# A recommender tower on one core: steps 0 and 1 in halves of their columns, part of step 2's first layer on VectorE, unread matmuls at both ends, tile 14's MLP in turn 31

## The chip, the cores and the metric

The kernel runs on one core of one Trainium2 chip. The metric is the device time of the whole kernel in microseconds (us). Before the change it is 1184.62 us, the median of three runs (1183.82 to 1184.74).

## What is computed

For each of 2048 samples, 32 rows of 16 numbers are looked up in 32 tables (`e`, 2048 x 32 x 16). Three layers of a compressed interaction network follow: each multiplies every pair of a field of `e` and a feature of the layer before, dimension by dimension, and contracts the pairs with weights to 64 features, with a ReLU. The sums over the 16 dimensions of the three layers, with 16 dense features, go through an MLP (208 to 512 to 256 to 1).

```python
x0 = e; xk = x0
for W in (W0, W1, W2):                       # W0: 32x32x64, W1 and W2: 32x64x64
    xk = relu(einsum('bmd,bhd,mhk->bkd', x0, xk, W))
    outs.append(sum(xk, axis=2))
h = concatenate([*outs, dense_ctx], axis=1)  # 2048 x 208
h = maximum(h @ W_top1 + b_top1, 0)
h = maximum(h @ W_top2 + b_top2, 0)
y = h @ W_top3
```

Everything is in float32.

## The kernel before

**Steps.** The batch is cut into 32 steps of 64 samples. In a step the 64 x 16 values of a field are 1024 columns (`COLS`), of which a matmul takes 512 (`BLK`). Two steps make a tile of 128 samples, for which the MLP runs once.

**Where the rows come from.** GpSimd gathers table rows by indirect DMA, 16 gathers for a step, into `x_rows`. SyncE (SP) stores them twice, one copy behind the other, in a scratch area in HBM (`store_x`, L184) and loads them from there, shifted by a number of fields for each group of 32 partitions: `q_tile` (the plain fields, four times, 0.52 MB) and eight tiles of `spread` (0.52 MB each), the first four with `load_a`, the last four with `load_b`. For step 0 the loads are shared by SP's and ScalarE's queues, and its and step 1's first four tiles each have a semaphore of their own.

**A layer.** All products of pairs are elementwise multiplications: a "chunk" is 128 pairs by 1024 columns. The first layer of a step (layer 0) has five chunks: four are `spread` tiles times `q_tile` (`p_l0`) and one holds the squares, 32 rows, made by ScalarE. Their products are made by VectorE for steps 0 and 1 and by GpSimd from step 2 on (two instructions of two chunks). Layers 1 and 2 have 16 chunks each, `spread` times the features of the layer before. VectorE makes 15 of them in groups of one to three (`GROUPS_L1`, `GROUPS_L2`) into a ring of ten slots (`p_dve`, `RING`), and waits for a slot to be consumed (`dve_used`); GpSimd makes chunk 7 (`p_pool`). TensorE contracts each chunk with two matmuls (`contract`, L624), one for each half of the columns, each with 64 output rows, one in the lower and one in the upper half of the accumulator's partitions. Every float32 matmul shows as two records.

**Between layers.** ScalarE moves the accumulator through a ReLU to `xa` (features in the order of chunks 0 to 7, `relu_a`), `xb` (chunks 8 to 15, `relu_b`), `x_s` (for GpSimd, `relu_s`) and `out_l` (for the sums, which VectorE makes with a reduction). `xa` and `xb` exist once, so that they are written when VectorE has passed the chunks that read them.

**The order.** There is no planner; the order on every engine is written out. Turn s holds layer 1 of step s and layer 2 of step s-1, and, inside layer 2, TensorE's layer 0 of step s+1 behind chunk `L0_AFTER` = 3. Step 1's layer 0 sits in layer 1 of step 0 behind chunk 10, step 2's in layer 2 of step 0 behind chunk 9. GpSimd's chunk is contracted behind chunk 9 (layer 1) or 11 (layer 2), for step 0 behind chunk 14. The MLP of tile t runs two turns and more after the tile's steps; that of tile 14 is placed in layer 2 of step 30 and of step 31. GpSimd's queue in a turn: first-layer products of step s+1, 4 gathers, its product of layer 2, 4 gathers, its product of layer 1 of the next step, 8 gathers. After the first 32 gathers it waits for `x1a_ready`, which says that ScalarE has written `xa` for step 0.

## Time and profile before

| | |
|---|---|
| median of three runs | 1184.62 us (1183.82 to 1184.74) |
| the profiled execution's own time | 1190.19 us |
| its span, first to last instruction | 1188.4 us |
| TensorE matmuls | 1121.7 us (94%), 5312 records |
| VectorE | 1119.2 us (94%) |
| ScalarE | 734.3 us (62%) |
| GpSimd | 913.9 us (77%) |
| loaded and stored | 167.25 MB, mean 141 GB/s |
| mean granted TensorE clock | 0.989 |

The profile is of one execution. PE is TensorE's matmuls, PEld its loads of weights, DVE is VectorE, ACT ScalarE, POOL GpSimd, SP SyncE; SPq and ACTq are DMA issues. Times are us from the span's start, and L542 is line 542 of the kernel. A merged row gives its start, its length, the engine, the line, the operation, the number of instructions, and in brackets how long the engine was idle before it and what ended that. A record of a matmul outlasts the start of the next one.

### The profile page before, as it was taken

What the parts mean: (1) busy time and instruction counts of PE and PEld (TensorE: products, weight loads), DVE (VectorE), ACT (ScalarE), POOL (GpSimd) and SP (SyncE); (2) the same over time, 40 slices, a digit from 0 to 9 for tenths busy, and PEclk for the clock granted to TensorE, in tenths of its full rate; (3) what the DMA queues carried; (4) which work ended last, traced back from release to release, by engine and by line L of the source; (5) the groups of instructions that cost most, each with busy time, mean ns of one, the idle gap of its engine ahead of it and who ended that gap; (6) DMA issues with size and microseconds to landing.
All of it is one profiled execution on the core that took longest, in us unless ns stands there. A gap on an engine that the chain in (4) does not pass through costs nothing.

```text
span 1188.4 us, 14675 instructions
## 1 busy us (share of the span) xinstructions
PE 1121.7 (94%) x5312; PEld 398.0 (33%) x5312; DVE 1119.2 (94%) x525; ACT 734.3 (62%) x1361; POOL 913.9 (77%) x640
## 2 busy tenths in 40 slices
PE   0489899999999999999999999999999999999997
PEld 0132223333333333333333333333333333333343
DVE  0488999999999999999999999999999999999994
ACT  0445667567656756765675676567567666756662
POOL 6568888888888888888888888888888888884300
PEclk9899999999999999999999999999999999999998
DMA  5885788767768876666787666678866667886100
GB/s 114 225 178 118 154 165 173 153 128 148 142 133 163 172 158 144 133 141 140 151 172 160 142 135 141 140 148 172 162 143 137 140 137 149 172 167 140 37 1 1
DMA packets 76472, 167.25 MB, mean 141 GB/s; under 512 B 22032, under 2 KB 39328, under 8 KB 76400
## 3 DMA queue, kind: packets, MB, share of 16 engines
q1 hardware_dynamic: 58704, 159.59, 63.8%
q0 software_dynamic: 16384, 4.23, 3.8%
q10 hardware_dynamic: 1312, 2.50, 0.8%
q8 instruction: 42, 0.69, 0.3%
q14 instruction: 30, 0.25, 0.1%
HBM read 157.86 MB, written 8.40 MB: 140 GB/s over the span
## 4 chain that ended last, share of the span: by engine, by line
PE 84%; issue 6%; DVE 2%; ACT 2%; DMA 1%; POOL 1%; another core or an unknown queue 1%; SPq 1%; ACTq 1%; DVEq 0%; POOLq 0%
PE acc L627 78%; PE acc L700 3%; DVE p_dve L542 2%; PE acc L686 1%; POOL x_rows L260 1%; PE acc L688 1%; DMA q_tile<-x_of_steps 1%; ACT xb L324 1%; PE acc L708 1%; ACTq L466 0%; SPq L197 0%; DMA x_rows<-in_table,ids_s 0%; SPq L225 0%; ACT xa L315 0%
## 5 line engine op out<-in xcount | busy, mean ns | idle before, releaser
L627 PE MATMUL acc<-p_dve,w_s 128*64 128x512 f32 x3840 | 859.6, 596 | 24.2 <-issue 12.7
L260 POOL DMA_INDIRECT x_rows<-in_table,ids_s x512 | 488.4, 954 | 152.5 <-issue 136.3
L542 DVE TENSOR_TENSOR p_dve<-spread,xb 128x3072 f32<-128x3072 f32 (+2 forms) x224 | 573.5, 2701 | 0.0
L542 DVE TENSOR_TENSOR p_dve<-spread,xa 128x2048 f32<-128x2048 f32 (+1 forms) x192 | 502.7, 2749 | 17.5 <-ACT xa L315 14.0
L627 PEld LDWEIGHTS acc<-p_dve,w_s 128*64 128x64 f32 x3840 | 272.1, 137 | 563.1 <-issue 489.4
L324 ACT ACTIVATE xb<-acc 32x512 f32<-32x512 f32 x512 | 288.8, 564 | 23.8 <-DVE p_dve L542 17.4
L272 POOL TENSOR_TENSOR p_l<-spread,q_tile 128x2048 f32<-128x2048 f32 x60 | 272.9, 4575 | 12.3 <-DMA q_tile<-x_of_steps 9.0
L315 ACT ACTIVATE xa<-acc 64x512 f32<-64x512 f32 x256 | 146.1, 571 | 183.9 <-DVE p_dve L542 98.2
L283 POOL TENSOR_TENSOR p_pool<-spread,x_s 128x1024 f32<-128x1024 f32 x64 | 152.4, 2381 | 85.4 <-PE acc L627 43.0
L627 PE MATMUL acc<-p_l,w_s 128*64 128x512 f32 (+1 forms) x640 | 153.1, 613 | 36.7 <-issue 36.7
L333 ACT ACTIVATE x_s<-acc 64x512 f32<-64x512 f32 x256 | 151.7, 593 | 8.2 <-ACT y_row L456 4.8
L342 ACT ACTIVATE p_l<-q_tile 32x1024 f32<-32x1024 f32 x32 | 33.8, 1056 | 116.7 <-DMA q_tile<-x_of_steps 116.7
L627 PEld LDWEIGHTS acc<-p_l,w_s 128*64 128x64 f32 (+1 forms) x640 | 40.9, 137 | 145.7 <-issue 143.7
L569 DVE TENSOR_REDUCE z<-out_l 128x32 f32<-128x512 f32 x96 | 70.0, 795 | 4.5 <-ACT out_l L408 4.5
L627 PE MATMUL acc<-p_pool,w_s 128*64 128x512 f32 x256 | 66.1, 592 | 0.0
L437 ACT ACTIVATE h<-acc,bt 128x128 f32<-128x128 f32 x64 | 18.3, 369 | 33.7 <-remote 25.8
L700 PEld LDWEIGHTS acc<-h,wt 128*128 128x128 f32 x256 | 31.4, 200 | 13.7 <-issue 12.2
L700 PE MATMUL acc<-h,wt 128*128 128x128 f32 x256 | 34.6, 291 | 1.2 <-ACT h L437 1.2
L627 PEld LDWEIGHTS acc<-p_pool,w_s 128*64 128x64 f32 x256 | 18.6, 137 | 36.4 <-issue 36.4
L583 DVE TENSOR_TENSOR p_l<-spread,q_tile 128x1024 f32<-128x1024 f32 x8 | 9.6, 1227 | 20.7 <-issue 19.1
L686 PE MATMUL acc<-z_all,wt 128*128 128x128 f32 x128 | 27.1, 294 | 2.0 <-ACT z_all L414 2.0
L408 ACT ACTIVATE out_l<-acc 128x512 f32<-128x512 f32 x32 | 19.2, 600 | 14.9 <-PE acc L627 14.8
(18 smaller groups left out, 160.2 us busy)
## 6 DMA issues: line engine op xcount, KB each, us to landing
spread<-x_of_steps SPq DMA_DIRECT2D x246, 512.0 KB
q_tile<-x_of_steps SPq DMA_DIRECT2D x126, 128.0 KB
x_rows<-in_table,ids_s POOLq DMA_INDIRECT x512
x_of_steps<-x_rows SPq DMA_DIRECT2D x64, 128.0 KB
spread<-x_of_steps SPq DMA_DIRECT2D x24, 128.0 KB
w_s<-in_w SPq DMA_DIRECT2D x2, 512.0 KB
spread<-x_of_steps ACTq DMA_DIRECT2D x8, 128.0 KB
spread<-x_of_steps ACTq DMA_DIRECT2D x2, 512.0 KB
```

The costliest lines, as they stand in the source:

```text
L260: nc.gpsimd.indirect_dma_start(out=x_rows[:, s % 2, i * DIM:(i + 1) * DIM], out_offset=None, in_=table, in_offset=bass.IndirectOffsetOnAxi ...
L272: nc.gpsimd.tensor_tensor(p_l0[:, c:c + 2, :], spread[:, s % 3, c:c + 2, :], q, ALU.mult).then_inc(l0_made, 2)
L283: nc.gpsimd.tensor_tensor(p_pool[:], spread[:, s % 3, POOL_CHUNK, :], x_s[:, layer - 1, :], ALU.mult).then_inc(pool_made, 1)
L315: last = nc.scalar.activation(xa[to:to + K, b * BLK:(b + 1) * BLK], acc[b * K:(b + 1) * K, :], ACT.Relu)
L324: last = nc.scalar.activation(xb[q * FIELDS:(q + 1) * FIELDS, b * BLK:(b + 1) * BLK], hi if q % 2 == 0 else lo, ACT.Relu)
L333: last = nc.scalar.activation(x_s[to:to + K, layer - 1, b * BLK:(b + 1) * BLK], acc[b * K:(b + 1) * K, :], ACT.Relu)
L342: nc.scalar.activation(p_l0[0:FIELDS, CP, :], q_tile[0:FIELDS, :], ACT.Square).then_inc(squares_made, 1)
L542: nc.vector.tensor_tensor(p_dve[:, to:to + n, :], spread[:, s % 3, tile:tile + n, :], over(x[:], n), ALU.mult).then_inc(dve_made, n)
L569: nc.vector.reduce_sum(z[:, s // 2 % 2, n, s % 2, :], out_l[:, n, :].rearrange("p (i d) -> p i d", d=DIM), AX_X).then_inc(z_made[n], 1)
L627: last = nc.tensor.matmul(acc[b * K:(b + 1) * K, :], w, prod[:, b * BLK:(b + 1) * BLK], start=start, stop=stop)
L686: nc.tensor.matmul(acc0[:, cols], wt1[:, 0, cols], z_all[:, 0, :], start=True, stop=False)
L700: last = nc.tensor.matmul(acc0[:, cols], wt2[:, k, cols], h1[:, k, :], start=(k == 0), stop=(k == H1 // P - 1))
```

## The change

- **Steps 0 and 1 in halves.** Samples are reordered so that the first 8 gathers of these steps bring the first 512 columns. Each half is stored, loaded (`load_half_by`, in rows half as long) and multiplied by VectorE by itself: one instruction for the first half, two for the second. TensorE contracts a half with one matmul per chunk (`layer0_half`), step 1's halves behind chunks 10 and 13. ScalarE squares each half and writes the first half of `xa` when that half is contracted. SP and ScalarE share the loads of step 1's second half and last four tiles.
- **Step 2's first layer.** VectorE makes its chunks 0 and 1 (`first_layer_of_2`), GpSimd chunks 2 and 3; TensorE takes it behind chunk 7 in place of 9.
- **GpSimd's order.** It makes 48 gathers without the wait for `x1a_ready`. Its chunk of layer 1 of step 0 is contracted behind chunk 5 of layer 1 of step 1.
- **Unread matmuls** (`keep_busy`): 4 before, 7 between and 8 behind the halves of step 0, then 4, 2 and 1 ahead of the last tile's three MLP layers.
- **Tile 14's MLP** follows chunks 6 and 12 of layer 2 of step 30 and chunk 1 of step 31. ScalarE collects its sums earlier, and evicts `mlp2` before `x2_b` of step 31.
- The last layer's last two chunks are separate instructions.

```diff
+GROUPS_LAST = [(0, 2), (2, 3), (5, 2), (8, 3), (11, 1), (12, 2), (14, 1), (15, 1)]
-POOL_AFTER_OF_0 = 14
+POOL_AFTER_L1_OF_0, POOL_AFTER_L2_OF_0 = 5, 14
-L0_OF_1_AFTER = 10
-L0_OF_2_AFTER = 9
+L0_OF_1_AFTER = 10, 13
+L0_OF_2_AFTER = 7
-LATE_MLP1_AFTER, LATE_MLP2_AFTER, LATE_MLP3_AFTER = 10, 14, 3
+BUSY_BEFORE, BUSY_BETWEEN, BUSY_BEHIND = 4, 7, 8
+BUSY_AT_END = 4, 2, 1
+LATE_MLP1_AFTER, LATE_MLP2_AFTER, LATE_MLP3_AFTER = 6, 12, 1
...
+        def load_half_by(engine, s, b, quads):
+            cols = slice(b * BLK, (b + 1) * BLK)
+            for q in quads:
+                engine.dma_start(q_tile[q * FIELDS:(q + 1) * FIELDS, cols],
+                                 scratch[s, 0:FIELDS, cols]).then_inc(half_q_loaded[s][b], 16)
+            for i, n, signal in ((0, NA, half_a_loaded[s][0]),) if b == 0 else \
+                    ((0, NA // 2, half_a_loaded[s][1]), (NA // 2, NA - NA // 2, a_loaded[s])):
+                for q in quads:
...
-            gathers(0, 2 * XI)
-            pool.wait_ge(x1a_ready, 1)
-            gathers(2 * XI, 3 * XI)
+            gathers(0, 3 * XI)
             product(0, 1)
             product(1, 1)
-            gathers(3 * XI, GATHERED_IN_TURN_0)
+            gathers(3 * XI, gathers_before(1))
...
+                if s < 2:
+                    for b in range(2):
+                        act.wait_ge(l0_used, 2 * s + b + 1)
+                        relu_a(acc0, x1a_ready, [b])
...
             x2_a(STEPS - 1)
             mlp1(TILES - 2)
+            mlp2(TILES - 2)
             x2_b(STEPS - 1)
-            mlp2(TILES - 2)
             out_2(STEPS - 2)
...
+            def first_layer_of_2():
+                dve.wait_ge(q_loaded, 16 * Q)
+                dve.wait_ge(a_loaded[2], 16 * Q)
+                dve.wait_ge(l0_used, 4)
+                n = CP // 2
+                nc.vector.tensor_tensor(p_l0[:, 0:n, :], spread[:, 2, 0:n, :],
+                                        over(q_tile[:], n), ALU.mult).then_inc(l0_made_by_dve, 2 * n)
...
+            def layer0_half(s, b):
+                if s > 0 and b == 0:
+                    pe.wait_ge(x1b_ready, s)
+                    pe.wait_ge(out_ready[0], s)
+                for c in CP, *range(CP):
...
+                    last = nc.tensor.matmul(acc0[b * K:(b + 1) * K, :], w0_s[0:rows, c, :],
+                                            p_l0[0:rows, c, b * BLK:(b + 1) * BLK],
+                                            start=c == CP, stop=c == CP - 1)
+                last.then_inc(l0_used, 1)
+
+            def keep_busy(acc, n):
+                for _ in range(n):
+                    nc.tensor.matmul(acc[0:K, :], w1_s[:, 0, :],
+                                     wt2[:, 0:BLK // H2, :].rearrange("p k n -> p (k n)"), start=True, stop=True)
...
+            keep_busy(acc2, BUSY_BEFORE)
+            layer0_half(0, 0)
+            keep_busy(acc2, BUSY_BETWEEN)
+            layer0_half(0, 1)
+            keep_busy(acc2, BUSY_BEHIND)
...
+            pe.wait_ge(out_ready[1], STEPS)
+            keep_busy(acc1[0], BUSY_AT_END[0])
             mlp1(TILES - 1)
+            keep_busy(acc1[0], BUSY_AT_END[1])
             mlp2(TILES - 1)
+            keep_busy(acc1[0], BUSY_AT_END[2])
             mlp3(TILES - 1)
```

## Rows read from the trace of the kernel before

**Rows 1.** The page, first part: busy us, share of the span, instructions.
```profile
PE 1121.7 (94%) x5312; PEld 398.0 (33%) x5312; DVE 1119.2 (94%) x525; ACT 734.3 (62%) x1361; POOL 913.9 (77%) x640
```

**Rows 2.** Timeline of VectorE in the middle: start, length, what [idle before].
```profile
598.21 7.86 DVE L542 TENSOR_TENSOR p_dve<-spread,xa 128x3072 f32<-128x3072 f32 x3
...
632.82 7.87 DVE L542 TENSOR_TENSOR p_dve<-spread,xa 128x3072 f32<-128x3072 f32 x3
```

**Rows 3.** Timeline of TensorE in the middle: an MLP layer and four chunks.
```profile
643.99 2.05 PE L700 MATMUL acc<-h,wt 128*128 128x128 f32 x16
...
649.46 3.60 PE L627 MATMUL acc<-p_dve,w_s 128*64 128x512 f32 x16
```

**Rows 4.** Timeline of VectorE, start of layer 1 of steps 0 to 3.
```profile
50.95 7.75 DVE L542 TENSOR_TENSOR p_dve<-spread,xa 128x3072 f32<-128x3072 f32 x3 [9.94 <-ACT xa L315]
...
76.66 7.75 DVE L542 TENSOR_TENSOR p_dve<-spread,xa 128x3072 f32<-128x3072 f32 x3 [4.05 <-ACT xa L315]
...
113.68 7.75 DVE L542 TENSOR_TENSOR p_dve<-spread,xa 128x3072 f32<-128x3072 f32 x3 [3.51 <-issue]
...
148.30 7.75 DVE L542 TENSOR_TENSOR p_dve<-spread,xa 128x3072 f32<-128x3072 f32 x3
```

**Rows 5.** Chain of waits at the end: start, length, what.
```profile
1163.89 10.48 PE acc L627 x48
...
1176.31 0.51 PE acc L686 x2
...
1181.05 3.79 PE acc L700 x16
```

**Rows 6.** Timeline of all engines, 0 to 70 us.
```profile
12.65 0.94 POOL L260 DMA_INDIRECT x_rows<-in_table,ids_s  x1 [0.30 <-issue]
...
22.63 0.94 POOL L260 DMA_INDIRECT x_rows<-in_table,ids_s  x1 [0.30 <-issue]
...
25.01 0.81 SPq L189 DMA_DIRECT2D x_of_steps<-x_rows  x2
...
27.23 0.79 SPq L225 DMA_DIRECT2D q_tile<-x_of_steps  x2
...
34.04 1.23 DVE L583 TENSOR_TENSOR p_l<-spread,q_tile 128x1024 f32<-128x1024 f32 x1 [18.64 <-issue]
...
39.79 1.23 DVE L583 TENSOR_TENSOR p_l<-spread,q_tile 128x1024 f32<-128x1024 f32 x1 [1.18 <-DMA spread<-x_of_steps]
...
43.45 0.14 PEld L627 LDWEIGHTS acc<-p_l,w_s 128*64 128x64 f32 x2 [0.60 <-issue]
...
48.55 2.32 ACT L315 ACTIVATE xa<-acc 64x512 f32<-64x512 f32 x4 [12.30 <-remote]
...
65.33 3.91 PE L627 MATMUL acc<-p_l,w_s 32*64 32x512 f32 x16
```

**Rows 7.** Timeline of ScalarE, 60 to 120 us.
```profile
74.25 2.32 ACT L315 ACTIVATE xa<-acc 64x512 f32<-64x512 f32 x4 [14.75 <-remote]
```

**Rows 8.** Windows: length, busy time per engine, granted clock, DMA share, GB/s.
```profile
57.00:70.00 13.00, 11.97 (x54) 3.56 (x52) 13.00 (x8) 2.48 (x4) 9.95 (x11) 1.00 1.06 212
...
74.10:77.50 3.40, 3.40 (x10) 1.49 (x8) 0.84 (x1) 3.18 (x6) 0.18 (x1) 0.51 0.25 82
...
1176.60:1188.40 11.80, 8.01 (x36) 6.75 (x35) 0.00 (x0) 2.04 (x7) 0.00 (x0) 0.50 0.00 0
```

**Rows 9.** Timeline of GpSimd, its products only.
```profile
79.73 2.37 POOL L283 TENSOR_TENSOR p_pool<-spread,x_s 128x1024 f32<-128x1024 f32 x1 [5.46 <-PE acc L627]
...
131.56 9.07 POOL L272 TENSOR_TENSOR p_l<-spread,q_tile 128x2048 f32<-128x2048 f32 x2
```

**Rows 10.** Timeline of all engines, 1138 to 1176 us.
```profile
1146.80 2.79 PE L627 MATMUL acc<-p_dve,w_s 128*64 128x512 f32 x12 [0.70 <-DVE p_dve L542]
...
1152.78 4.60 ACT L324 ACTIVATE xb<-acc 32x512 f32<-32x512 f32 x8
...
1159.71 3.65 PE L627 MATMUL acc<-p_dve,w_s 128*64 128x512 f32 x16 [0.70 <-ACT out_l L408]
```

More of the change, by code:

```diff
@@ L142, in build_kernel @@
         q_loaded = sem("q_loaded")
-        tile_loaded = [[sem(f"tile{i}_of_step{s}_loaded") for i in range(NA - 1)] for s in range(2)]
+        half_gathered = [[sem(f"half{b}_of_step{s}_gathered") for b in range(2)] for s in range(2)]
+        half_q_loaded = [[sem(f"half{b}_of_step{s}_q_loaded") for b in range(2)] for s in range(2)]
+        half_a_loaded = [[sem(f"half{b}_of_step{s}_a_loaded") for b in range(2)] for s in range(2)]
         a_loaded = [sem(f"a_loaded{u}") for u in range(3)]
@@ L258, in gather @@
                 if i == 0 and s >= 2:
-                    pool.wait_ge(x_stored, 32 * (s - 1))
+                    pool.wait_ge(x_stored, stored(s - 2) if s >= 4 else 64 * (s - 1))
                 nc.gpsimd.indirect_dma_start(
@@ L310, in _, with relu_a @@
         def _(act):
-            def relu_a(acc, signal):
-                for b in range(2):
+            def relu_a(acc, signal, halves=range(2)):
+                for b in halves:
                     for to in 0, K:
@@ L316, in relu_a @@
                                                     acc[b * K:(b + 1) * K, :], ACT.Relu)
-                last.then_inc(signal, 1)
+                if halves[-1] == 1:
+                    last.then_inc(signal, 1)
             def relu_b(acc, signal):
@@ L351, in x1_a @@
                     act.wait_ge(dve_made, dve_from(s - 2, 2) + POOL_CHUNK)
-                relu_a(acc0, x1a_ready)
+                if s < 2:
+                    for b in range(2):
+                        act.wait_ge(l0_used, 2 * s + b + 1)
+                        relu_a(acc0, x1a_ready, [b])
+                else:
+                    act.wait_ge(l0_used, 2 * (s + 1))
+                    relu_a(acc0, x1a_ready)
             def x1_s(s):
@@ L376, in x2_a @@
                 act.wait_ge(dve_used, dve_from(s, 1) + CD)
+                if s == 0:
+                    act.wait_ge(pool_used, 1)
                 if s + 1 < STEPS:
@@ L611, in _ @@
                     for c, n in GROUPS_L2:
+                        if s == 1 and c == L0_OF_2_AFTER + 1:
+                            first_layer_of_2()
                         layer2(s - 1, c, n)
-            for c, n in GROUPS_L2:
+            for c, n in GROUPS_LAST:
                 if c == NT:
@@ L645, in layer0 @@
-                    contract(acc0, w0_s[0:rows, c, :], p_l0[0:rows, c, :], c == CP, c == CP - 1
-                             ).then_inc(l0_used, 1)
+                    if c == CP:
+                        pe.wait_ge(squares_made, 2 * (s + 1))
+                    elif s == 2 and c < CP // 2:
+                        pe.wait_ge(l0_made_by_dve, l0_by_dve(2))
+                    else:
+                        pe.wait_ge(l0_made, l0_by_pool(s) - CP + c + 1)
+                    last = contract(acc0, w0_s[0:rows, c, :], p_l0[0:rows, c, :], c == CP, c == CP - 1)
```

237 lines of the change are left out of this document (141 added, 96 removed).

## The prediction, made before the changed kernel was run

> **What bounds the kernel now.** I read the page's first part, then the timeline of VectorE, then ScalarE's and TensorE's rows at both ends, then GpSimd's. The page names no bound: TensorE and VectorE are both busy 94% of the span [rows 1], and the chain of waits runs mostly over TensorE. The timeline decides it. In the middle VectorE starts layer 1 of one step at 598.21 and of the next at 632.82, so a step lasts 34.61 us, and no row between shows idle time [rows 2]. TensorE needs less: a chunk is four matmul records (two passes of two column halves), and 16 of them take 3.60 us with the overhang of the last, some 0.17, so a chunk costs 0.86 [rows 3]; 37 chunks are 31.8 us, and the MLP adds some 4.5 us per two steps. So VectorE sets the pace, TensorE follows with under 1 us of slack, and GpSimd (16 gathers of 1.25 us, 9.1 us of first-layer products, two products of 2.4 us, some 33.9 us) is nearly full as well. The middle is untouched by the diff, apart from fewer increments of l0_used. What can move is (a) when VectorE enters each of the first layers and (b) what follows its last product.
>
> VectorE enters layer 1 of steps 0 to 3 at 50.95, 76.66, 113.68 and 148.30, with idle times of 9.94, 4.05 and 3.51 before the first three and none after [rows 4]. The last product begins at 1167.99; TensorE ends at about 1174.36, the program 14.0 later [rows 5].
>
> **S, the start of layer 1 of step 0.** Now: the 16th gather is issued at 22.63, its rows are stored at 25.01, loads start at 27.23, the first product at 34.04, the fourth at 39.79; TensorE's last load of weights is at 43.45, and ScalarE begins x1_a at 48.55, 4.2 us after the matmuls should be over (44.3) [rows 6]. This lag is a hold on TensorE's completions: its waits are over and nothing else precedes ScalarE.
> After: (1) first half. The 8th gather (12.65) is 10.0 us before the 16th, so the store is at 15.0, the load at 17.2. 1.05 MB (q and tile 0) took 6.8 us (27.23 to 34.04), the other three tiles of 0.52 MB 5.75, 1.9 each [rows 6]; half of q and of four tiles is 1.31 MB, 6.8 and half a tile more, 7.7 us: 24.9. Its product has 2048 elements, 2.2 us: 27.1. (2) second half. The gathers aren't faster: stored from 25.0, loads from 27.2; 0.79 MB in 5.9, by 33.1, the rest by 35.1, last product at 36.3 (before 41.0). (3) TensorE. A half is ONE matmul per chunk, without a partner in the other column half. The nearest row is the MLP: 8 unpaired matmuls on 128 columns of data in 2.05 us with the overhang [rows 3], under 0.25 each; 512 columns are four times that: 0.86 to 1.0, I take 0.86. So an unpaired half costs what both halves cost now; lower bound 0.43. At half clock it is double, as mlp2 shows at the end (3.79 [rows 5]). First half: four matmuls after 27.1, 3.4 to 6.8 us, to 30.5 to 33.9. Then seven unread ones, in order, 6.0 us: to 36.5 to 39.9, which covers the second half's products. Then five, 4.3: 40.8 to 44.2. I take 42.5: the split and the fillers give back most of the 4.7 us that the loads won. (4) Lag. GpSimd no longer stops for x1a_ready, so gathers and bulk loads run on together, as around 43 us. Bounds 0 and 7.7 (layer 0 of step 1: its first chunk runs at 65.33 and is done by 66.2 [rows 6]; TensorE's records end at 70.9, and ScalarE starts at 74.25 after 14.75 us of waiting [rows 7], so the lag is 3.4 at the last chunk and at most 8.1 less the handover at the first); I take 3.5, near the first row. (5) ScalarE has only half of x1_a left, 1.2 instead of 2.4.
> S = 42.5 + 3.5 + 1.2 = 47.2 (bounds 42.1 and 53), against 50.95.
>
> **From S to step 1 (T).** VectorE alone: 7.7, sum 0.6, 3.3, half of step 1 2.3, 3.3, other half 2.3, 2.2 = S+21.7. TensorE is later: chunks 8 to 10 after S+11.5, to S+14.1; half, five matmuls, to S+18.4; chunks 11 to 13 to S+21.0; half to S+25.3; ScalarE's half 1.2 and handover: T = S+26.8 = 74.0. Now it is 25.7, the same path with lag. The split adds 8.6 us of TensorE in all, and takes VectorE's place here. The 48th gather is issued at 22.63+32x1.25 = 62.6 plus delays, so no gathers and no lag at T. Data: one queue moves 212 GB/s [rows 8]. The last four tiles of step 0 end at about 44.5, then come a store, 1.31 MB to 55, a store, and 1.31 MB by two queues to about 64.7, needed at S+18.3 = 65.5.
>
> **Steps 2 and 3.** The GpSimd chunk of layer 1 of step 0 is read after chunk 5 of step 1, T+9.4, so GpSimd's next product starts at T+9.5, now at T+3.1 (79.73) [rows 9]. Twelve gathers in place of eight; its half of step 2's first layer from T+26.9 to T+31.5 (4.5 saved), VectorE's half 2.2 at T+24.7, behind it (8,3) to (14,2). TensorE has layer 0 of step 2 by T+33.3, ScalarE by T+35.8, VectorE by T+35.6: layer 1 of step 2 at T+35.9 = 109.9 (now T+37.0). A product waits 1.3 for pool_used; first-layer products of step 3 start at T+58.1, now T+54.9 (131.56) [rows 9], while layer 2 of step 1 starts at T+54.1, now T+55.2. Ten slots of the ring then run full: (14,2) wants chunk 5 consumed at T+70.0, ready at T+68.3; stall 1.7 to 2.0. Layer 1 of step 3 at T+72.4 = 146.4, now 148.30: gain 1.9. GpSimd's own turn is 33.5, so it catches up and nothing more is lost.
>
> **End.** mlp1 of tile 14 goes after chunk 6 (1146.1), where TensorE is idle 0.70 until 1146.80: to 1148.1; chunks 8 to 12 and GpSimd's, 5.15, to 1153.2; mlp2 to 1155.2. But ScalarE now does mlp2's eviction BEFORE x2_b: 1155.2+0.63, x2_b 4.60 to 1160.4, out_2 to 1161.1. TensorE's last layer starts on out_2, now at 1159.71 [rows 10]: 1.35 later, and TensorE has no gap after it, so its end moves to 1175.7. VectorE waits 0.9 for the same out_2 and has that in hand. Splitting (14,2) changes nothing, TensorE being behind.
> Unread matmuls: mlp1 to mlp3 run at half clock now (granted 0.50 from 1176.6 on [rows 8]), 3.5 + 3.79 + 1.0 [rows 5]. Four fillers end 3.45 after the last layer, the sums are there at 1.95; mlp1 then takes 1.98 and ends at 5.43 instead of 5.47. Two fillers cost 0.5, mlp2 saves 1.8, one filler costs 0.2, mlp3 saves 0.5: 1.65. Net of both: 0.3 gained.
>
> **Sum.** 1.9 + 0.3 = 2.2. The profiled execution took 1190.19 (span 1188.4), so 1188.0; that run lies 5.6 above the median shown, which I carry over: 1182.4.
>
> **A rule on halves.** Rows 3 show the four records of a pair of 64-column matmuls in 0.86 us; none is unpaired.
> The Trainium skill (TensorEngine Tiling (Array Packing), Overview) says that the array can act as independent smaller ones, up to twice as fast when one dimension is 64 or less; by that a half alone leaves the other array idle and costs 0.86. Without it, at 0.43, S would be 2.1 and T another 3.5 earlier, 1176.8. The trace has the paired rows on its side, no run here shows the other.
>
> **Rivals.**
> A (0.22): the hold doesn't return and the clock is full from 27 us. S = 42.1, T 68.9, also the limit of the data; step 3 gains 7, sum 7.3: 1177.3. For: after the gathers end the rows show completions told at once. Against: both causes of the hold stay. Unpaired halves at 0.43 go here.
> B (0.24), slower: the hold is the longer one because gathers now run on: S = 42.5+7.7+1.2 = 51.4, T = 78.2, step 3 at 150.6, 2.3 lost, and at the end the idle stretch of C: 1.7 less 0.3. Together 3.7 slower, 1188.3. It decides from S = 49.1 on, that is a lag over 5.4. GpSimd's later chain makes it worse. Against: TensorE has only one increment per half to tell.
> C (0.14): as forecast at the start, but TensorE's idle stretch from 1157.8 to 1161.1 lets the clock fall, as at 74.1 to 77.5 (0.51) after gaps [rows 8]; two chunks at double price, 1.7: 1184.1, no difference.
> The skill's page TensorE: Matmul & The Clock Gate (Why this matters for your kernels) asks for no idle gaps between bursts; it speaks for C.
> Forecast (0.40): 1179.8 to 1184.
>
> **How the numbers follow.** A measurement of this kernel tells about 0.2%, 2.4 us, from no change. The forecast lies at that edge: 0.20 faster, 0.20 same. With A faster is 0.42, and 0.01 for C with an early start, 0.43; same 0.33; slower is B, 0.24. The range goes to A's and B's values, 1176 to 1188.5.
>
> **What would show it.** VectorE's layer 1 of step 0 at 47 and of step 1 at 74; layer-0 matmuls in 0.86 steps; no idle before 110 and a short stall near 142; GpSimd's products of step 3 after layer 2 of step 1 has begun; out_2 of step 30 some 1.4 later relative to VectorE; granted clock 1.0 to the end. Wrong if step 1 starts before 70 or after 78, or if the middle's 34.61 moves.

## The result, and the profile after

The changed kernel takes 1194.97 us (median of 4 runs, 1194.19 to 1196.11) against 1184.68 for the kernel before on the same chip: ratio 1.0085, interval 1.0073 to 1.0098. It is 10.3 us slower; 1182.4 was forecast. Its profiled execution took 1195.44 (span 1193.6).

The page's first part, beside [rows 1]: TensorE is 29 us busier (the unread matmuls, and the halves of layer 0 that run without a partner), VectorE hardly at all.

```profile
PE 1150.6 (96%) x5364; PEld 404.2 (34%) x5364; DVE 1121.8 (94%) x525; ACT 733.9 (61%) x1363; POOL 915.0 (77%) x639
```

VectorE's timeline, the starts of layer 1 of steps 0 to 3, beside [rows 4]. Against the profile of before, steps 0 and 1 begin 5.7 and 3.9 us earlier, step 2 at the same time, and step 3 is 3.5 us later.

```profile
45.28 7.75 DVE L621 TENSOR_TENSOR p_dve<-spread,xa 128x3072 f32<-128x3072 f32 x3 [6.96 <-ACT xa L381]
72.75 7.75 DVE L621 TENSOR_TENSOR p_dve<-spread,xa 128x3072 f32<-128x3072 f32 x3 [4.22 <-issue]
...
113.62 7.75 DVE L621 TENSOR_TENSOR p_dve<-spread,xa 128x3072 f32<-128x3072 f32 x3 [5.15 <-ACT xa L381]
...
151.76 3.35 DVE L621 TENSOR_TENSOR p_dve<-spread,xa 128x3072 f32<-128x3072 f32 x1 [0.32 <-PE acc L725]
```

GpSimd's timeline, its products only, beside [rows 9]. The second product waits 12.16 us for TensorE to free the one product buffer, and everything behind it in the queue is late: its half of step 2's first layer, and the first layer of step 3 at 135.43.

```profile
84.27 2.38 POOL L350 TENSOR_TENSOR p_pool<-spread,x_s 128x1024 f32<-128x1024 f32 x1 [12.16 <-PE acc L725]
103.02 4.54 POOL L339 TENSOR_TENSOR p_l<-spread,q_tile 128x2048 f32<-128x2048 f32 x1
...
118.16 2.37 POOL L350 TENSOR_TENSOR p_pool<-spread,x_s 128x1024 f32<-128x1024 f32 x1 [3.42 <-PE acc L725]
135.43 9.06 POOL L339 TENSOR_TENSOR p_l<-spread,q_tile 128x2048 f32<-128x2048 f32 x2
```

TensorE's timeline shows who waits for it: layer 0 of step 2 stands still for 4.90 us until GpSimd's half is there, and layer 0 of step 3 for 2.34. In the profile of before TensorE stops in neither (106.57 and 139.32, 20 records without idle time).

```profile
107.62 1.12 PE L725 MATMUL acc<-p_l,w_s 128*64 128x512 f32 x2 [4.90 <-POOL p_l L339]
...
144.54 3.35 PE L725 MATMUL acc<-p_l,w_s 128*64 128x512 f32 x8 [2.34 <-POOL p_l L339]
```

The end, all engines, beside [rows 10]. ScalarE evicts the late MLP (L529) first, for that waits until TensorE has made mlp2, and only then begins x2_b of step 31 (L391); TensorE's last layer, which waits for out_2 (L490), stands idle for 3.23 us instead of 0.70.

```profile
1156.77 2.05 PE L828 MATMUL acc<-h,wt 128*128 128x128 f32 x16
...
1158.86 0.62 ACT L529 ACTIVATE h<-acc,bt 128x128 f32<-128x128 f32 x2 [6.14 <-PE acc L828]
1159.51 4.59 ACT L391 ACTIVATE xb<-acc 32x512 f32<-32x512 f32 x8
1164.13 0.60 ACT L490 ACTIVATE out_l<-acc 128x512 f32<-128x512 f32 x1
...
1164.78 3.01 PE L725 MATMUL acc<-p_dve,w_s 128*64 128x512 f32 x8 [3.23 <-ACT out_l L490]
```

In windows (length, busy time of each engine, granted clock, DMA share, GB/s; beside [rows 8]) the clock is half behind that idle time and full at the very end, where it was half before:

```profile
1166.10:1168.60 2.50, 2.50 (x8) 0.34 (x5) 2.50 (x1) 1.50 (x3) 1.51 (x1) 0.50 0.00 0
...
1183.60:1186.10 2.50, 2.50 (x17) 1.74 (x16) 0.00 (x0) 0.00 (x0) 0.00 (x0) 1.00 0.00 0
```

**Where the time is.** The span falls into stretches, cut at VectorE's start of layer 1 of step 1 (T), of step 3, and at the end. All later tables use them. The table gives microseconds of each profiled execution:

| kernel | T | T to step 3 | step 3 to end | span |
|---|---|---|---|---|
| before, profile shown | 76.66 | 71.64 | 1040.10 | 1188.4 |
| changed, forecast | 74.0 | 72.4 | 1039.8 | 1186.2 |
| changed, measured | 72.75 | 79.01 | 1041.84 | 1193.6 |

The forecast missed by -1.25, +6.6 and +2.0: 7.4 us in all, and 1188.0 + 7.4 = 1195.4 is the profiled time. The other 5.1 us of the miss in the median come from the carrying over: the profile of before lay 5.6 above its median, that of the changed kernel only 0.5.

### The profile page after: what moved, and what is told of

It is laid out like the page before. It is cut to its first block, busy times and chain, and to the rows that moved or that the text cites. A ratio compares the mean times of both kernels' runs of the same rounds, so it can differ in the third digit from the quotient of the medians.

```text
span 1193.6 us, 14793 instructions
## 1 busy us (share of the span) xinstructions
PE 1150.6 (96%) x5364; PEld 404.2 (34%) x5364; DVE 1121.8 (94%) x525; ACT 733.9 (61%) x1363; POOL 915.0 (77%) x639
## 4 chain that ended last, share of the span: by engine, by line
PE 87%; POOL 3%; issue 3%; DVE 3%; DMA 2%; ACT 1%; SPq 0%; ACTq 0%; DVEq 0%; POOLq 0%
PE acc L725 79%; PE acc L828 3%; DVE p_dve L621 3%; POOL x_rows L326 2%; PE acc L758 1%; PE acc L814 1%; PE acc L816 1%; PE acc L767 1%; DMA q_tile<-x_of_steps 1%; POOL p_l L339 1%; PE acc L836 1%; DMA spread<-x_of_steps 0%; DMA x_rows<-in_table,ids_s 0%; POOL p_pool L350 0%; ACT xb L391 0%
## 5 line engine op out<-in xcount | busy, mean ns | idle before, releaser
L326 POOL DMA_INDIRECT x_rows<-in_table,ids_s x512 | 494.2, 965 | 146.3 <-issue 131.7
L621 DVE TENSOR_TENSOR p_dve<-spread,xb 128x3072 f32<-128x3072 f32 (+2 forms) x225 | 566.2, 2574 | 3.0 <-PE acc L725 2.9
L621 DVE TENSOR_TENSOR p_dve<-spread,xa 128x2048 f32<-128x2048 f32 (+1 forms) x192 | 495.4, 2635 | 16.6 <-ACT xa L381 12.1
L391 ACT ACTIVATE xb<-acc 32x512 f32<-32x512 f32 x512 | 288.8, 564 | 61.6 <-DVE p_dve L621 55.4
L339 POOL TENSOR_TENSOR p_l<-spread,q_tile 128x2048 f32<-128x2048 f32 x59 | 268.3, 4574 | 11.5 <-DMA q_tile<-x_of_steps 9.2
L725 PE MATMUL acc<-p_l,w_s 32*64 32x512 f32 (+1 forms) x600 | 143.1, 612 | 7.2 <-POOL p_l L339 7.2
L725 PEld LDWEIGHTS acc<-p_l,w_s 32*64 32x64 f32 (+1 forms) x600 | 37.9, 137 | 109.0 <-issue 97.6
L648 DVE TENSOR_REDUCE z<-out_l 128x32 f32<-128x512 f32 x96 | 62.6, 678 | 7.4 <-ACT out_l L490 7.4
L767 PE MATMUL acc<-wt,w_s 128*64 128x512 f32 x52 | 25.1, 629 | 15.4 <-DVE w_s L688 15.4
L828 PEld LDWEIGHTS acc<-h,wt 128*128 128x128 f32 x256 | 29.8, 191 | 13.0 <-issue 12.2
L490 ACT ACTIVATE out_l<-acc 128x512 f32<-128x512 f32 x32 | 19.1, 597 | 15.5 <-PE acc L725 15.4
L665 DVE TENSOR_TENSOR p_l<-spread,q_tile 128x1024 f32<-128x1024 f32 (+1 forms) x6 | 9.5, 1581 | 19.8 <-DMA spread<-x_of_steps 19.8
L496 ACT ACTIVATE z_all<-z 64x64 f32<-64x64 f32 x96 | 24.2, 253 | 5.0 <-DVE z L648 3.8
```

The lines of the kernel that those rows point to most:

```text
L326: nc.gpsimd.indirect_dma_start(out=x_rows[:, s % 2, i * DIM:(i + 1) * DIM], out_offset=None, in_=table, in_offset=bass.IndirectOffsetOnAxi ...
L339: nc.gpsimd.tensor_tensor(p_l0[:, c:c + 2, :], spread[:, s % 3, c:c + 2, :], q, ALU.mult).then_inc(l0_made, 2)
L391: last = nc.scalar.activation(xb[q * FIELDS:(q + 1) * FIELDS, b * BLK:(b + 1) * BLK], hi if q % 2 == 0 else lo, ACT.Relu)
L621: nc.vector.tensor_tensor(p_dve[:, to:to + n, :], spread[:, s % 3, tile:tile + n, :], over(x[:], n), ALU.mult).then_inc(dve_made, n)
L648: nc.vector.reduce_sum(z[:, s // 2 % 2, n, s % 2, :], out_l[:, n, :].rearrange("p (i d) -> p i d", d=DIM), AX_X).then_inc(z_made[n], 1)
L725: last = nc.tensor.matmul(acc[b * K:(b + 1) * K, :], w, prod[:, b * BLK:(b + 1) * BLK], start=start, stop=stop)
```

## The experiments

The kernel before has medians from 1184.7 to 1189.6 on different chips, a wider spread than most effects that are asked about here. So kernels are compared on one chip, through its runs of the kernel before, and by the stretches above. The chips are called A to E, in the order of use.

### Chip A: the two parts that were suspected

**e0_before_again**: the kernel before, unchanged.

> The kernel before, unchanged, for a second profile. Its first profiled execution took 1190.19 us, its median is 1184.7. Theory 1 (that profile shows a typical course): again about 1190 under the profiler, VectorE's layer 1 of step 0 near 50.9 and of step 1 near 76.7, with TensorE's completions told 3 to 4 us late. Theory 2 (that execution was late by chance at the start): 1184 to 1186, and the first layers begin some 5 us earlier, with less lag.

It took 1186.91, between the two expected times; the starts fit theory 2. Its timeline of VectorE, against [rows 4]:

```profile
47.18 7.75 DVE L542 TENSOR_TENSOR p_dve<-spread,xa 128x3072 f32<-128x3072 f32 x3 [5.74 <-ACT xa L315]
70.38 3.35 DVE L542 TENSOR_TENSOR p_dve<-spread,xa 128x3072 f32<-128x3072 f32 x1
...
145.16 7.75 DVE L542 TENSOR_TENSOR p_dve<-spread,xa 128x3072 f32<-128x3072 f32 x3 [0.32 <-PE acc L627]
```

ScalarE began x1_a at 44.77, at once behind the matmuls; the lag of 4.2 us that my step (4) rested on isn't there. Step 1 starts at 70.38, before the changed kernel's 72.75. So most of the start that the change was to win had been lost in the one profile that I read, and another execution of the same kernel has it. Half of it doesn't last: T is 6.3 us earlier than in that profile, but T to step 3 takes 74.78 in place of 71.64.

**e1_pool_chunk_back**: the changed kernel, GpSimd's chunk of step 0's layer 1 contracted where it was.

```diff
-POOL_AFTER_L1_OF_0, POOL_AFTER_L2_OF_0 = 5, 14
+POOL_AFTER_L1_OF_0, POOL_AFTER_L2_OF_0 = 14, 14
...
-                             c == CL - 1 and s > 0).then_inc(dve_used, 1)
-                if s == 1 and c == POOL_AFTER_L1_OF_0:
-                    pool_chunk(0, True)
+                             c == CL - 1).then_inc(dve_used, 1)
+                if s == 0 and c == POOL_AFTER_L1_OF_0:
+                    pool_chunk(0, False)
```

> The changed kernel with one edit: GpSimd's chunk of layer 1 of step 0 is contracted behind chunk 14 of that layer again, instead of behind chunk 5 of step 1. Theory P (GpSimd's chain, held up by that chunk, is what starts steps 2 and 3 late): GpSimd's product of step 1 starts near 75 in place of 84.3, its first-layer products of step 2 near 94 in place of 103, VectorE's idle times of 5.15 and 3.2 us go, median 8.4 lower, about 1186.5. Rival H (halves and unread matmuls cost it, GpSimd's wait is hidden behind them): under 2 us lower, 1193 or more.

1185.74 (10 runs), 9.2 us faster than the changed kernel (by medians; the kernel before had 1184.96 here and 1184.68 beside the changed one), 1.0006 of before (0.9993 to 1.0019); 8.4 were expected. GpSimd's timeline: the product comes 2.4 us behind T instead of 11.5, the first layer of step 3 at T + 56.0 instead of T + 62.7. (The 3.99 us of the third row are taken up in the last section.)

```profile
76.07 2.37 POOL L350 TENSOR_TENSOR p_pool<-spread,x_s 128x1024 f32<-128x1024 f32 x1 [5.90 <-ACT x_s L400]
93.33 4.58 POOL L339 TENSOR_TENSOR p_l<-spread,q_tile 128x2048 f32<-128x2048 f32 x1
98.82 3.99 POOL L350 TENSOR_TENSOR p_pool<-spread,x_s 128x1024 f32<-128x1024 f32 x1 [0.92 <-ACT x_s L400]
...
129.65 9.09 POOL L339 TENSOR_TENSOR p_l<-spread,q_tile 128x2048 f32<-128x2048 f32 x2
```

And VectorE's, T and step 3: 70.65 us apart instead of 79.01.

```profile
73.66 7.75 DVE L621 TENSOR_TENSOR p_dve<-spread,xa 128x3072 f32<-128x3072 f32 x3 [5.92 <-issue]
...
144.31 7.75 DVE L621 TENSOR_TENSOR p_dve<-spread,xa 128x3072 f32<-128x3072 f32 x3 [0.32 <-PE acc L725]
```

**e2_evict_after_xb**: the changed kernel, ScalarE's order at the end as before.

```diff
-            mlp2(TILES - 2)
             x2_b(STEPS - 1)
+            mlp2(TILES - 2)
```

> The changed kernel with one edit: ScalarE evicts the second MLP layer of tile 14 behind x2_b of step 31 again. Theory E (that order makes TensorE wait 3.2 us for out_2, and the wait lets the clock fall for 3.4 us): TensorE's last layer starts 2.6 us earlier, no stretch at 0.5 there, median 4.3 lower, about 1190.7. Rival (TensorE would wait for chunks or for the MLP instead, since its matmuls were moved as well): under 1 us lower.

1190.97 (5 runs), 4.0 us faster than the changed kernel, 1.0047 of before (1.0031 to 1.0063). In the timeline x2_b waits for VectorE only, and TensorE's last layer follows in time:

```profile
1155.51 4.59 ACT L391 ACTIVATE xb<-acc 32x512 f32<-32x512 f32 x8 [3.05 <-DVE p_dve L621]
...
1161.34 0.60 ACT L490 ACTIVATE out_l<-acc 128x512 f32<-128x512 f32 x1 [0.58 <-PE acc L725]
...
1161.99 1.94 PE L725 MATMUL acc<-p_dve,w_s 128*64 128x512 f32 x8 [0.70 <-ACT out_l L490]
```

**e3_both**: both edits.

> Both edits of the two runs before. If P and E hold and are independent, as they sit at opposite ends: 12.7 lower than the changed kernel, about 1182.2, which is 2.5 below the kernel before. If either gain is taken back by the middle (VectorE and TensorE in step there), less than the sum of the two.

1183.01 (10 runs, 1182.62 to 1183.97), 0.998 of before (0.9968 to 0.9991): 12.0 us under the changed kernel, where the parts alone gave 13.2. It is 2.0 us under the kernel before on this chip. On chips C and D the same kernel with GpSimd's pause (below) isn't faster than before.

### Chip B: single parts, and something else

All four are e3 with one edit:

```diff
# e4
-BUSY_BEFORE, BUSY_BETWEEN, BUSY_BEHIND = 4, 7, 8
+BUSY_BEFORE, BUSY_BETWEEN, BUSY_BEHIND = 0, 0, 0
# e5
-BUSY_AT_END = 4, 2, 1
+BUSY_AT_END = 0, 0, 0
# e6: TensorE's second half of step 1's first layer
-                    if s == 0 and c in L0_OF_1_AFTER:
-                        layer0_half(1, L0_OF_1_AFTER.index(c))
+                    if s == 0 and c in (10, 11):
+                        layer0_half(1, c - 10)
# e7: GpSimd makes all of step 2's first layer
-                for c in (0, 2) if s > 2 else (2,):
+                for c in 0, 2:
...
-                        if s == 1 and c == L0_OF_2_AFTER + 1:
-                            first_layer_of_2()
...
```

**e4_no_start_fillers**

> The kernel of e3_both (GpSimd's chunk back, eviction behind x2_b; 1183.01 us) without the 19 unread matmuls at the start. Theory F (the seven between the halves stand in front of the second half, whose products are ready at 38.6 while TensorE starts on it at 39.4 and ends at 44): layer 1 of step 0 starts at 41.5 to 43.2 instead of 45.3, and of step 1 up to 3.6 earlier, median 1179.5 to 1181. Rival C (they keep the clock full through layer 1 of step 0; without them it runs at 0.5 there, TensorE falls behind and tells its chunks late): step 1 no earlier than 72.8, median 1183 or more.

**e5_no_end_fillers**

> The kernel of e3_both without the seven unread matmuls at the end. The three last MLP layers run at a granted clock of 0.5; by the prediction's term 1.65 us are lost, median 1184.6. Rival (the fillers in front of each layer cost what the clock saves): no difference, 1183.0.

**e6_half_after_11**

> The kernel of e3_both with TensorE's second half of step 1's first layer behind chunk 11 instead of chunk 13; VectorE's order is unchanged. Theory U (unpaired halves make TensorE late for step 1: it begins that half at 66.8 though its last product is there at 66.1): the half ends at about 68.3, step 1 begins at 69.8 instead of 72.8, median 3 lower, 1180.0. Rival (the 3 us are given back at layer 1 of step 2, which waits for GpSimd and for data): 1182.5 or more.

**e7_no_share_of_2**

> The kernel of e3_both with all four products of step 2's first layer on GpSimd again, still read behind chunk 7. Theory W (GpSimd then loses its present wait of 4.7 us for pool_used instead of being later, and VectorE is spared 2.2 us): layer 1 of step 2 starts at about 106.3 instead of 108.4, of step 3 at 142, median 1181.5. Rival (GpSimd's 4.5 us more push step 3's first layer back, as in the changed kernel): a stall of VectorE near 140 and 1186 or more.

They took 1199.26, 1210.67, 1206.53 and 1212.26, 1.010 to 1.019 of before on this chip, and the loss lies ahead of T, which stood at 87.5, 99.8, 88.5 and 99.9. In e5 and e7, whose edits touch nothing there, VectorE waited 34 to 35 us for the first x1_a. In e4 and e6 the first x1_a came at 45.5 to 45.6, but VectorE stood still for over 11 us later in step 0, for chunks that TensorE got to late. e3 itself wasn't run on this chip; its control follows on chip C. As tests of their own edits the times say nothing, and e4's and e6's questions stay unanswered here; two stretches say a little. From T to step 3 e7 takes 72.38 and e5 70.66, which would make VectorE's share of step 2's first layer worth 1.7 us; but e4 takes 73.21 and e9 below, which is e3 again, 73.76, so that this isn't shown. From step 3 to the end e5 takes 1038.20 and e3 1037.71: the fillers at the end would be worth 0.5.

### Chip C: the hold

Rival B's mechanism had come back, larger than I had priced it. By "the hold" I mean here that TensorE's work is done or told late while GpSimd issues gathers. **e8_both_and_pause** is e3 with one wait put back:

```diff
-            gathers(0, 3 * XI)
+            gathers(0, 2 * XI)
+            pool.wait_ge(x1a_ready, 1)
+            gathers(2 * XI, 3 * XI)
```

> The kernel with both parts put back (GpSimd's product of step 0's first layer contracted behind chunk 14 of step 0; ScalarE writes x2_b of step 31 ahead of the eviction of the late MLP), and in it GpSimd waits for ScalarE's first x1_a again before the gathers of turn 3, as before the change. Theory G (a long unbroken row of gathers can hold back what ScalarE hears of TensorE's matmuls): step 0's layer 1 starts on VectorE at 45 to 48 us and no idle stretch of VectorE ahead of step 1's layer 1 is over 6 us, on whatever chip it runs; gathers then resume behind ScalarE's x1_a (about 44 us). On a chip where the control without the pause shows the hold (VectorE idle for 11 to 35 us between 37 and 72 us), this kernel is 14 to 28 us faster than the control; on a chip where the control shows none, the two are within 1.5 us. Rival (the hold is the chip's, whatever GpSimd does): both show the idle stretch and the same time.

**e9_both_again** is e3, the control.

> The control: the kernel with both parts put back, unchanged, GpSimd issuing its 48 gathers without a pause. 0.998 of the kernel before on a chip like the first one (no hold); 1.01 to 1.02 of it where the hold shows, with VectorE idle until about 72 us.

The control took 1211.17 (1.0200 of before, 1.0183 to 1.0218), with the pause 1189.31 (12 runs, 1.0016, 1.0003 to 1.0029): 21.9 us, inside the 14 to 28 expected. The control's timeline: TensorE's last half matmul starts at 44.04 and fillers follow; GpSimd issues its last gather at 63.82; ScalarE hears of the matmuls at 71.90, 7 us after the gathers and 27 after the matmul. Not only the telling is late: the fillers wait for nothing, yet the last two records of them stand behind idle times of 2.30 and 3.02 us.

```profile
44.04 0.59 PE L758 MATMUL acc<-p_l,w_s 128*64 128x512 f32 x1
...
55.69 1.01 PE L767 MATMUL acc<-wt,w_s 128*64 128x512 f32 x1 [3.02 <-issue]
...
63.82 0.95 POOL L326 DMA_INDIRECT x_rows<-in_table,ids_s  x1 [0.30 <-issue]
...
71.90 1.16 ACT L381 ACTIVATE xa<-acc 64x512 f32<-64x512 f32 x2 [36.60 <-remote]
```

With the pause the gathers stop at 44.72, ScalarE starts at 49.53 and the gathers go on behind it:

```profile
44.72 0.94 POOL L326 DMA_INDIRECT x_rows<-in_table,ids_s  x1 [0.30 <-issue]
...
49.53 1.16 ACT L383 ACTIVATE xa<-acc 64x512 f32<-64x512 f32 x2 [13.31 <-remote]
...
50.95 0.94 POOL L326 DMA_INDIRECT x_rows<-in_table,ids_s  x1 [5.29 <-ACT xa L383]
```

I had expected step 0's layer 1 at 45 to 48 us and no idle stretch over 6; it starts at 50.78, and VectorE is idle for 12.2. What is left is a lag like that of [rows 6], 6.1 us (49.53 behind a matmul that ended at 43.45), with the pause too.

**e10_pause_no_fillers**: e8 without any fillers (unread matmuls).

> The pause is in, and the unread matmuls at both ends (19 at the start, 7 at the end) are out; the computation is whole. If the fillers at the start hide a slow clock there (my step in the prediction counted TensorE's end of the second half at 42.5 with them), step 0's layer 1 starts later than in the kernel with the pause and the fillers: TensorE would run the first half's 8 matmuls and part of the second's at half clock, but these wait for products (33.9 and 37.3 us) more than for TensorE, so I expect 0 to 1.7 us there. At the end the fillers save at most 1.65 us by the clock. Theory: 1.5 to 3 us slower than the kernel with pause and fillers. Rival (the fillers are worth nothing, since TensorE waits there in any case): within 0.6 us.

1193.98 (12 runs, 1188.73 to 1197.59; 1.0044, 1.0027 to 1.0061): 4.7 us slower than e8, more than the 1.5 to 3 expected, and not for the reason given. Without fillers TensorE is done with step 0's first layer at 40.76 instead of 43.5, and ScalarE begins 2.3 us earlier than in e8. Timeline:

```profile
36.65 1.93 PE L760 MATMUL acc<-p_l,w_s 128*64 128x512 f32 x4 [1.68 <-issue]
...
38.83 1.93 PE L760 MATMUL acc<-p_l,w_s 128*64 128x512 f32 x4 [0.24 <-issue]
...
47.20 1.16 ACT L383 ACTIVATE xa<-acc 64x512 f32<-64x512 f32 x2 [11.97 <-issue]
```

The time is lost behind it, on the way to T, 84.89: while the gathers of turn 3 run, TensorE's matmuls of step 1's first half come one or a few at a time, from 62.92 to 74.67. Whether the missing fillers brought that on isn't shown. From step 3 to the end it takes 1037.26 (e8 1037.74), so the fillers at the end are worth -0.5 here, +0.5 on chip B: nothing.

**e11_pause_half_after_11**: e8 with e6's edit.

> The pause is in, and TensorE contracts the second half of step 1's first layer behind chunk 11 of step 0's layer 1 instead of chunk 13 (VectorE's products for it keep their place behind chunk 13, so TensorE would wait for them at 66.3 us with chunks 12 and 13 queued behind: this tells what the place costs). If TensorE's end sets the start of step 1's layer 1 (theory), it ends no earlier, since the products come at 66.3 us: step 1 starts at 72 to 73.5 us and the time is within 0.8 us of the kernel with the pause. Rival (the chunks behind the half hold the ring of VectorE's buffers): 1 to 3 us slower.

1186.75 (13 runs; 0.9993, 0.9982 to 1.0004), 2.6 us faster than e8, where I had expected no gain. Its profile fell on one of its two long runs (1194.3, T at 83.84). That one shows what e4, e6 and e10 show: step 0 starts on time (45.37), and then, with the pause over, matmuls come one or a few at a time while GpSimd issues its gathers, so that VectorE waits 12.44 us:

```profile
65.79 2.43 PE L727 MATMUL acc<-p_dve,w_s 128*64 128x512 f32 x3 [1.02 <-issue]
...
71.62 3.35 DVE L623 TENSOR_TENSOR p_dve<-spread,xb 128x3072 f32<-128x3072 f32 x1 [12.44 <-PE acc L727]
```

The 2.6 us are nearly found in a profile of the same kernel on chip D (e12, below). In e8 VectorE is done with step 1's second half at 70.13, but TensorE, with chunks 11 to 13 ahead of it, begins it at 73.02. In e12 it is done at 69.83 and TensorE begins at 70.31, so that S to T takes 25.75 instead of 28.11. The products were there when TensorE came to them, so its order was what step 1 waited for. This rests on one profile each, from two chips. First e8, then e12:

```profile
73.02 3.30 PE L760 MATMUL acc<-p_l,w_s 32*64 32x512 f32 x7
...
70.31 3.36 PE L760 MATMUL acc<-p_l,w_s 32*64 32x512 f32 x7
```

### Chip D: after again, the end alone, the chunk in between

**e13_end_alone**: the kernel before with the part at the end (GROUPS_LAST, the MLP of tile 14 behind chunks 6, 12 and 1, its moves in turn 31, the 7 fillers), ScalarE's order as before.

```diff
-LATE_MLP1_AFTER, LATE_MLP2_AFTER, LATE_MLP3_AFTER = 10, 14, 3
+BUSY_AT_END = 4, 2, 1
+LATE_MLP1_AFTER, LATE_MLP2_AFTER, LATE_MLP3_AFTER = 6, 12, 1
...
```

> The kernel before with the part at the end alone: the MLP of tile 14 goes behind chunks 6 and 12 of step 30's layer 2 and chunk 1 of step 31's, its blocks are moved in turn 31, the last group of VectorE's layer 2 is cut in two, and 7 unread matmuls stand ahead of the last three products; ScalarE's order (x2_b of step 31 ahead of the second eviction) is kept as before. My prediction put fillers at -1.65 and the later start of the last layer at +1.35; with that order kept, TensorE waits 0.7 instead of 3.2 us for ScalarE, so the later start should be gone: 1 to 2 us faster than before. Rival (the end is set by VectorE's last sums, which nothing here makes earlier but the cut group): within 0.5 us of before.

1187.90 against 1186.60 (1.0006, 0.9998 to 1.0015): no gain in the time. Yet from step 3 to the end it takes 1037.71, 2.4 us less than the profile of before (1040.10; e0 1039.94). Its T, 76.74, has the lag, which nothing of this edit touches. Whether the kernel before has it less often on this chip isn't shown; what the 2.4 us of the stretch are worth in a median stays open.

**e15_after_again**: the changed kernel.

> The changed kernel unchanged. Where no hold shows: 1.0085 of before, as it was. Theory G (the hold comes with gathers issued without a pause, on some chips): on a chip where the kernel without the pause shows VectorE idle for over 10 us between 37 and 72 us, 1.02 to 1.03 of before. Rival: the hold came with the two parts put back, and this kernel keeps 1.0085 on any chip.

1222.13 (1.0281, 1.0254 to 1.0308). So the changed kernel is 1% slower than before where TensorE isn't held up, and nearly 3% where it is.

**e14_chunk_behind_0**: the changed kernel, the chunk contracted behind chunk 0 of step 1.

```diff
-POOL_AFTER_L1_OF_0, POOL_AFTER_L2_OF_0 = 5, 14
+POOL_AFTER_L1_OF_0, POOL_AFTER_L2_OF_0 = 0, 14
```

> The changed kernel with GpSimd's chunk of step 0's layer 1 contracted behind chunk 0 of step 1's layer 1 instead of chunk 5. Theory P (GpSimd's one product buffer is freed later, so its whole queue and with it the first layer of step 3 moves): GpSimd's product of step 1 starts at about 5 us behind the start of step 1's layer 1 (11.5 in the changed kernel, 2.4 with the chunk behind chunk 14 of step 0), and of the 9.2 us some 9.2 x (11.5 - 5) / (11.5 - 2.4) = 6.6 come back: step 3's layer 1 starts about 72.5 us behind step 1's (79.0 and 70.7). Rival Q (any place in step 1's row costs the same, by the wait of the row itself): within 1 us of the changed kernel.

1220.61: nothing came back where 6.6 us were expected, though GpSimd's half of step 2's first layer did start earlier (T + 24.4 instead of T + 30.3; its product of step 1 at T + 7.1, where I had expected 5). T to step 3: 78.16. The rival's number nearly came out (1222.13 for e15), and its reason was wrong, as the last two runs show.

**e12_pause_half_11_again**: e11 on this chip.

> The kernel with both parts put back, GpSimd's pause ahead of the gathers of turn 3, and the second half of step 1's first layer behind chunk 11 on TensorE, unchanged: the best so far on a chip with the hold (0.9993 of before there). Where no hold shows: 0.997 to 0.999 of before, some 2 us faster, as the kernel without the pause was on the first chip.

1186.59 (0.9994, 0.9986 to 1.0003): level with before as on chip C, not 2 us faster. This chip isn't one without the hold (e14, e15), and the profile has the lag (ScalarE begins x1_a at 49.25, behind a matmul that ended at 45.18; T 76.24).

### Chip E: what ate the gain of e14

**e16_chunk_0_pause** is e14 with GpSimd's pause; **e17_share_earlier** has VectorE make its share of step 2's first layer a group earlier:

```diff
-                        if s == 1 and c == L0_OF_2_AFTER + 1:
+                        if s == 1 and c == 5:
                             first_layer_of_2()
```

> The changed kernel with GpSimd's chunk of step 0's layer 1 contracted behind chunk 0 of step 1's, and with GpSimd's pause ahead of the gathers of turn 3, which takes the hold away. Both theories: VectorE's half of step 2's first layer starts at 24 to 25 us behind the start of step 1's layer 1, at the same time as GpSimd's, and takes 7 to 9 us; step 3's layer 1 starts 77 to 79 us behind step 1's.

> The same, and VectorE makes its half of step 2's first layer one group earlier (ahead of the group that begins with chunk 5 of step 0's layer 2 instead of chunk 8), some 2.3 us earlier, so that it is nearly or wholly done before GpSimd begins. TensorE reads it at the same place. Theory V (a product of VectorE with both operands in SBUF stands still while GpSimd runs a product; those with xa or xb in PSUM do not): it takes 2.3 us, TensorE's wait of 4.8 us ahead of chunk 8 falls to under 1 us, step 3's layer 1 starts 72 to 74 us behind step 1's, and the kernel is 4 to 6 us faster than its control. Rival (the late part is GpSimd's own half, read by the same TensorE instructions): TensorE waits as long, and the time is within 1 us of the control.

1193.55 and 1189.56, 4.0 us apart, the low end of the 4 to 6 expected. e16's timeline:

```profile
96.35 4.54 POOL L339 TENSOR_TENSOR p_l<-spread,q_tile 128x2048 f32<-128x2048 f32 x1
96.78 8.56 DVE L676 TENSOR_TENSOR p_l<-spread,q_tile 128x2048 f32<-128x2048 f32 x1
...
100.83 2.36 POOL L350 TENSOR_TENSOR p_pool<-spread,x_s 128x1024 f32<-128x1024 f32 x1
105.39 0.29 PEld L727 LDWEIGHTS acc<-p_l,w_s 128*64 128x64 f32 x4 [6.04 <-DVE p_l L676]
105.39 5.52 PE L727 MATMUL acc<-p_l,w_s 128*64 128x512 f32 x16 [5.16 <-DVE p_l L676]
```

VectorE's product lasts 8.56 us and ends 2.15 behind GpSimd's second product (100.83 + 2.36 = 103.19): it stood still until both were over, and TensorE waited 5.16 for it. In e17 it is ahead of them and takes 2.29:

```profile
95.46 2.29 DVE L676 TENSOR_TENSOR p_l<-spread,q_tile 128x2048 f32<-128x2048 f32 x1
...
98.58 4.57 POOL L339 TENSOR_TENSOR p_l<-spread,q_tile 128x2048 f32<-128x2048 f32 x1
...
101.87 4.66 PE L727 MATMUL acc<-p_l,w_s 32*64 32x512 f32 x20
```

T to step 3 is 77.72 and 72.47: of the 8.4 us between chunk 5 (79.0) and chunk 14 (70.65), 6.5 come back with the earlier place once the collision is out of the way, as theory P had it. What e17's second edit does to the changed kernel by itself, with the chunk behind 5, wasn't run; there the product that it moves collides with nothing (2.29 us at 97.39).

## Why the prediction was wrong, by its steps

**S.** Step (4), the lag of 3.5, wasn't there (44.04 for x1_a behind a matmul begun at 43.41); TensorE's end came at 43.8 (43.41 and one record of 0.43) instead of 42.5, since the first half's four chunks took 5.9 us, at a granted clock of 0.50 from 27.3 to 30.8. S = 45.28 against 47.2. The timeline of the start:

```profile
27.33 6.09 PE L758 MATMUL acc<-p_l,w_s 128*64 128x512 f32 x8 [4.59 <-DVE p_l L665]
...
42.55 0.59 PE L758 MATMUL acc<-p_l,w_s 128*64 128x512 f32 x1
42.61 0.59 PE L767 MATMUL acc<-wt,w_s 128*64 128x512 f32 x1
...
43.41 0.59 PE L758 MATMUL acc<-p_l,w_s 128*64 128x512 f32 x1
44.04 1.16 ACT L381 ACTIVATE xa<-acc 64x512 f32<-64x512 f32 x2 [9.37 <-PE acc L758]
```

Step (3), an unpaired half costs 0.86 per chunk, held: each chunk is two records, and the second half's records start 0.46 apart from 39.36 to 42.55, nearly all alone, and 0.43 from there on, with a filler beside each. That a filler in the other column half runs beside such a record (it starts 0.06 behind it) was new. But the fillers between the halves, which I let "cover the second half's products", hold TensorE 2.7 us past them (e8 against e10).

**T - S** was 27.47 against 26.8, by the steps given. T itself, 72.75, was 1.25 early. That it came so near is in part luck: the lag was counted 3.5 too long, and TensorE's end (1.3) and T - S (0.7) too short.

**T to step 3 is the step that failed**, "layer 1 of step 3 = T+72.4", measured T + 79.0. The sentence "GpSimd's next product starts at T+9.5" was 2.0 short: TensorE is idle for 2.97 us ahead of step 1's row and then runs at half clock for 3.4 us, which costs 1.7 and which I hadn't counted there. The window behind that idle time:

```profile
76.70:80.10 3.40, 3.40 (x12) 0.96 (x10) 3.40 (x2) 3.33 (x7) 0.00 (x0) 0.50 1.00 257
```

Twelve gathers took 16.4 us instead of 15 (one took 2.44), so GpSimd's half was ready at T + 34.8 instead of T + 31.5. I wrote that TensorE "has layer 0 of step 2 by T+33.3", as if it came when the half was ready; it came at T + 30.0 (107.62 - 4.90 - 72.75), so what I had as an idle time of 1.5 became one of 4.9. Behind it came another half-clock stretch (granted clock 0.53 from 107.5 to 111), and step 2 was 5.0 later than forecast, step 3 6.6. I also wrote that "GpSimd's own turn is 33.5, so it catches up and nothing more is lost". It hasn't caught up when the first layer of step 3 is read: TensorE waits 2.34 us for GpSimd at 144.54, and VectorE then 2.90 for ring slots. e1 shows the size of the whole: 9.2 us in the medians, 8.4 in the stretch. The Trainium skill (TensorE: Matmul & The Clock Gate, Why this matters for your kernels) advises against long idle gaps between bursts of matmuls. The trace agrees, and shows the clock fall behind gaps shorter than the page names: 2.97 us here, and 2.11 in e1, which was granted 0.58 behind it. The measurement decides.

**End.** I had out_2 of step 30 1.35 later; measured against step 3 TensorE's last layer starts 1.61 later (1164.78 - 3.46 = 1161.32 against [rows 10]). Rival C, with a chance of 0.14, then happened on top: 0.50 in the window behind, and from its start to its end the last layer took 1.6 us longer than in e2. The fillers' term came out as 1.46 (last sum to end 11.92 against 13.38) where 1.65 was forecast, but it isn't the fillers that earn it: without them the stretch is the same within 0.5 (e5, e10). With ScalarE's order kept, the end gains 2.4 over before (1037.7 against 1040.1), in place of losing 1.7. That order costs 4.0 us (e2). What of the end's other parts earns the 2.4, the earlier MLP or the divided group, wasn't taken apart.

**The rivals.** A was right that the lag doesn't return, but its S and T were 3.2 and 3.9 us early and its end wrong. B's mechanism, TensorE held up while gathers run on, is real, on chips B, C and D, where T came 15 to 28 us later than on chip A and I had a lag of at most 7.7. It isn't what made the recorded 1194.97: there the profile shows no lag at all. None of them had the GpSimd queue as its place; B named it without a price. That was the gap: I priced the wait and the queue behind it, found 3.2 us, and took the slack ahead of TensorE's reading for more than it was.

**The base.** The 10.3 us between the medians are the cost of the change. The two profiles show only half of it (5.2), because that of before, 1190.19, was an execution with the lag. Against e0's span the changed kernel's is 8.5 us longer: 2.4 ahead of T, 4.2 from T to step 3, 1.9 behind. So the 3.7 us that I won at S were hardly a gain: against e0 S is 1.9 us earlier (45.28 against 47.18) and T 2.4 later, since S to T takes 27.47 instead of 23.20. That fits the step by which the halves cost TensorE time there; a run with only step 1 whole again would test it, and wasn't made. e0 is one profile, 2 us above its median. Had I read a second profile, or taken the 5.6 us between profile and median as a sign that the start was late in it, I would have seen this before the forecast.

## What to carry to other kernels

When a contraction that frees a single buffer is moved later in one engine's order, follow the queue of the engine that fills the buffer to its next two products and ask when each is read; moving it back was worth 9 us here, and what was left of the change, with ScalarE's order put back too, at most 2. At an engine that evicts for two consumers, the eviction that the critical one needs goes first (4 us). And where a profile lies 0.5% above the median, find out in which stretch before using that stretch as what a change can win.
